# Six quads of the last stage in plain fp32 on an x that GpSimd splits afterwards, in a graph kernel on one Trainium2 core

## The chip, the cores and the metric

The kernel runs on one core of a Trainium2 chip. The metric is the device time of one execution in microseconds, and it is compared by the median of several runs.

## The reference, cut to what matters

The input is x (8192 x 128) and an adjacency matrix (8192 x 8192, fp32, 256 MB), of which about one entry in 256 is not zero; the kernel treats it as dense.

```python
d   = 1 / sqrt(sum(A, axis=-1))
z   = leaky_relu((d[:, None] * (A @ (d[:, None] * x))) @ W1 + b1, 0.1)
d2  = maximum(sq[:, None] + sq[None, :] - 2 * (z @ z.T), 0)     # sq = sum(z * z, axis=-1)
S   = exp(-sqrt(d2 + 1e-10) / 2)                                # kept for the 4 nearest of a row, else 0
A2  = S + A
e   = 1 / sqrt(sum(A2, axis=-1))
out = layernorm(x + (e[:, None] * (A2 @ (e[:, None] * x))) @ W2 + b2)
```

So A is multiplied twice, the second time with rows of x that are scaled by sums which need the four nearest neighbours of every row. The second product falls apart into A times the scaled x, and four gathered rows per row.

## The kernel before, in words

A row block b and a column block h are 512 wide (b, h from 0 to 15). A **quad** (b, h) is the 512 x 512 piece of A that they share, laid out for TensorE in DRAM, 1 MB and one DMA. A **tile** is 128 rows of x; a column block has four tiles, a **group** eight tiles, that is two column blocks.

Stages 1 and 2 (to about 1027 us in the span) form the row sums and the first product, and z. Stage 3 takes the 64 tiles one after the other: TensorE makes the 128 x 8192 scores of a tile, ScalarE copies them into SBUF, VectorE finds the eight largest and their places (`v.max`, `v.max_index`, semaphore `placed`). The rows of x of a group whose neighbours are known are scaled ("xg"), split into two parts that TensorE multiplies at its faster fp32r rate (a high half, rounded, and a low half, the rest), and written to DRAM three times: as fp32 (`xs_dram`), as high halves (`xh_dram`) and as low halves (`xl_dram`). The second product of row blocks 0 to 8 ("lights") with column blocks 0 to 13 is done beside stage 3; its sums lie in `acc_dram`.

**The last stage** does what is left of the second product: 124 quads in a fixed order, `tail`, made by `plan_tail` (line 115), u being the position in it. Row blocks 9 to 15 are "heavies" with 14 or 16 quads each, and the lights have two quads each (column blocks 14 and 15, h >= LAST). Row block 9 comes first; its first `OPEN_T` = 6 quads stand alone, then a light quad and a heavy one alternate. After that, two lights are put into each heavy block, at h = 5 and h = 10.

A quad takes one of two ways (function `quad`, line 961):
- **in halves**: ScalarE rounds the whole quad into `ah_t` (`round_t`, line 1194, operation at line 1197), VectorE subtracts to get the rest `al_t` in two parts (`rest_t`, line 1670, operation at line 1675), and TensorE does twelve fp32r matmuls (lines 987, 989, 993) with the high and low halves of x, which SP has loaded back from `xh_dram` and `xl_dram` (`load_xs`, line 721). The rests of the first two quads (`BY_POOL`) are made by GpSimd (line 1448).
- **plain**: four fp32 matmuls straight on the loaded quad (line 977). Before, these are the 32 quads of column blocks 14 and 15, which use the last group's `xg` in SBUF and wait until it is scaled (`xg_ok`).

Quads arrive in `RAW_T` = 7 buffers: SP issues the load of position u when the quad at u - 7 is done (`load_t`, line 715). The seven first loads and the halves of groups 0 to 2 are issued from line 727 on, behind waits for the last tile of stage 3; the others from line 741 on. In this trace the loads land in the order in which they are issued.

The last group's scale is made while the stage opens, in a chain over two engines, whose links stand at fixed positions of the loops: VectorE makes the distances (`last_chain_a`, line 1634), ScalarE takes root and exponential (`s_of_distances`, line 1099, at u = 2), VectorE the sums (`last_near_sums`, line 1643, at u = 3), ScalarE their root (`root_of_sums`, line 1106, at u = 3), VectorE the Newton step and the scaling of xg (`last_scale_of_rows` and `scale_last_xg`, at u = 4). GpSimd then writes xg to `xs_dram` (line 1453) and, when that has landed, issues 256 gathers of 128 rows with 512 bytes each (line 1464): 16 for each row block f in the order `FIN`, into three sets of buffers. ScalarE weighs them with the neighbours' S (`weigh`, line 1204, operation at line 1208), VectorE adds them, TensorE adds them to the block's sums and multiplies with W2, and so on to the layer norm. All that is tied to positions `FIN_AT`: ScalarE weighs the four parts of block f at u = FIN_AT[f] - 7 to FIN_AT[f] - 4. Each engine goes through its loop over u in order, so what waits at one position holds up all that stands behind it on that engine.

Of the kernel before, what the change touches and what calls it, by code (L numbers as in the profile page):

```python
# [39 lines left out]
RAW_T, HIGH_T = 7, 3  # L40
BY_POOL = 2
GX = 3
# [4 lines left out]
FIN_AT = (22, 28, 34, 41, 48, 55, 62, 69, 76, 83, 90, 97, 103, 109, 115, 123)  # L47
OPEN_T, SUM_AFTER, ACC_AT = 6, 4, (9, 20, 40)
SLOT = TB * BC
# [65 lines left out]
def plan_tail():  # L115

    lights = [(b, h) for b in LIGHTS for h in range(LAST, B)]
    quads = [(HB, h) for h in range(OPEN_T)]
    for h in range(OPEN_T, LAST):
        quads += [lights.pop(0), (HB, h)]  # L120
    quads += [(HB, h) for h in range(LAST, B)]
    for b in HEAVIES[1:]:
        for h in range(first_h(b), B):
            if h in (B // 3, 2 * B // 3) and lights:
                quads.append(lights.pop(0))
            quads.append((b, h))
    return quads


def build(nc, x, at, W1, b1, W2, b2, consts, out, xs_dram, xh_dram, xl_dram, acc_dram):  # L130
# [48 lines left out]
    with ctx:  # L179
# [114 lines left out]
        al_t = [sb(f"al_t{k}", [P, TB, BC], F32R, at=where) for k, where in enumerate(low_at)]  # L294

        def low_tile(t):

            return xsl[:, t] if t < (G - 2) * GT else xsh[:, t + GT]

# [97 lines left out]
        s_acc_x = sem("s_acc_x")  # L397
        acc_seeded = sem("acc_seeded")
        rnd_t = sem("rnd_t")
        al_pool = sem("al_pool")  # L400
        al_dve = sem("al_dve")
# [127 lines left out]

        plain = [h >= LAST for b, h in tail]  # L530
        halved = [u for u in range(len(tail)) if not plain[u]]
        place_of = {u: n for n, u in enumerate(halved)}

        def wait_rest(eng, u, part_=RESTS - 1):

            if place_of[u] < BY_POOL:
                eng.wait_ge(al_pool, place_of[u] + 1)
            else:
                eng.wait_ge(al_dve, RESTS * (place_of[u] - BY_POOL) + part_ + 1)

# [112 lines left out]
        def _(sp):  # L653
# [61 lines left out]
            def load_t(u):  # L715
# [3 lines left out]
                sp.dma_start(raw_t[u % RAW_T], at[b, h]).then_inc(ld_t[u % RAW_T], 16)  # L719

            def load_xs(g):
                low = g if g < G - 2 else G - 1
# [3 lines left out]

            sp.wait_ge(s_split, 32 * (G - 1))
            sp.wait_ge(placed, T - 1)
            for g in range(2):
                load_t(g)  # L730
                sp.wait_ge(gram, NE * (T - 1) + g + 1)
                load_xs(g)
            load_t(2)
            sp.wait_ge(gram, NE * T)
            load_t(3)
            load_xs(2)
            load_t(4)
            sp.wait_ge(prodb, pieces_before(G - 1))
            for u in range(5, RAW_T):
                load_t(u)  # L740
            for u in range(RAW_T, len(tail)):
                for g in range(3, G - 1):
                    if u == max(RAW_T, tail.index((HB, g * GT // TB)) - 1):
                        load_xs(g)
# [15 lines left out]
        def _(pe):  # L760
# [200 lines left out]
            def quad(u):  # L961
# [11 lines left out]
                if plain[u]:  # L973
                    pe.wait_ge(xg_ok, chain_of(G - 1, False))
                    pe.wait_ge(ld_t[u % RAW_T], 16 * (u // RAW_T + 1))
                    for k in range(TB):
                        i = pe.matmul(bank, xg[:, (h * TB + k) % GT], raw_t[u % RAW_T][:, k],  # L977
                                      start=from_zero and k == 0, stop=last and k == TB - 1,
                                      skip_group_check=True)
                    i.then_inc(prod_t, 1)  # L980
                    return
                pe.wait_ge(s_xs[h * TB // GT], 32)
                n = place_of[u]
                pe.wait_ge(rnd_t, n + 1)
                for k in range(TB):
                    t = h * TB + k
                    pe.matmul(bank, xsh[:, t], ah_t[n % HIGH_T][:, k], start=from_zero and k == 0, stop=False,  # L987
                              skip_group_check=True)
                    pe.matmul(bank, low_tile(t), ah_t[n % HIGH_T][:, k], start=False, stop=False, skip_group_check=True)
                for k in range(TB):  # L990
                    if k % (TB // RESTS) == 0:
                        wait_rest(pe, u, k * RESTS // TB)
                    i = pe.matmul(bank, xsh[:, h * TB + k], al_t[u % RAW_T][:, k], start=False, stop=False,
                                  skip_group_check=True)
# [33 lines left out]
        def _(act):  # L1028
# [211 lines left out]
            for u in range(len(tail)):  # L1240
                if not plain[u]:
                    round_t(u)
                for i, b in enumerate(ROWS_X):
                    if u == (FIN_AT[FIN.index(b - 2)] + 3 if b - 2 in HEAVIES else FIN_AT[0] - 8):
                        seed_heavy(i)
                if u == BY_POOL:
                    s_of_distances(G - 1)
                if u == BY_POOL + 1:
                    root_of_sums(G - 1)
                    act.wait_ge(placed, T)  # L1250
# [21 lines left out]
        def _(pool):  # L1272
# [198 lines left out]
        def _(v):  # L1471
# [308 lines left out]
```

## Time and profile before

| what | value |
|---|---|
| time, median of 3 runs (lowest, highest) | 2683.36 us (2681.94, 2683.89) |
| time of the profiled execution, and its span | 2679.84 us, 2678.0 us |
| last stage in the span | from 2233.6 us (first load) to the end, 444 us |
| busy share of the whole span | PE 92%, DVE 87%, ACT 60%, POOL 45% |
| granted clock of TensorE, mean of the span | 0.979 |

Times of rows count from the start of the span. PE is TensorE, DVE is VectorE, ACT is ScalarE, POOL is GpSimd, SP the engine that issues the loads (its queue is SPq). A granted clock of 1.00 is 2.4 GHz. DMA share is the mean busy share of the core's 16 DMA engines; it can come out a little over 1. "Idle before <-releaser" is the time in which the engine stood still just before an operation, and what ended it. Engine shares are means over stages with different limits, so the last stage is read from its own windows and timelines.

### The profile page before, as it was taken

Reading aid. Unit: us, or ns where it says so; the run is one execution under the profiler, and the core shown is the slowest. Engines: PE = TensorE matmul, PEld = TensorE weight load, DVE = VectorE, ACT = ScalarE, POOL = GpSimd, SP = SyncE. Lnnn points to the kernel's source line nnn. Section 1 sums busy time; section 2 is a strip of 40 time slices with the busy share of each in tenths; the row PEclk is TensorE's granted clock in tenths of the full one; section 3 lists DMA queues with packets and bytes.
Section 4 is the critical chain, followed back from the end, with each engine's and each line's share of the span. In section 5 each row is a group of like instructions: output and inputs, shape, how many; then the busy total and the mean of one; then the engine's idle time right before and its main releaser. Section 6 shows DMA issues by size and latency. Waiting matters only on the chain.

```text
span 2678.0 us, 29073 instructions
## 1 busy us (share of the span) xinstructions
PE 2456.8 (92%) x9356; PEld 1710.4 (64%) x9356; DVE 2319.3 (87%) x1411; ACT 1606.8 (60%) x1905; POOL 1193.2 (45%) x987
## 2 busy tenths in 40 slices
PE   0467999999999999899999999999999998899998
PEld 0133444444577777577778787877878775577776
DVE  7998889976788887999999999989999877488887
ACT  0000000000377776899998989889898876477776
POOL 0000000000000000067788888878787895777772
PEclk9678999999999999999999999999999999999999
DMA  9999999997699981035565555545555568999996
GB/s 383 421 405 402 399 421 421 421 421 291 236 374 345 341 329 52 0 114 170 147 170 147 168 149 141 175 135 177 146 173 148 168 179 320 398 400 402 400 402 244
DMA packets 147948, 718.58 MB, mean 268 GB/s; under 512 B 19024, under 2 KB 26960, under 8 KB 86608
## 3 DMA queue, kind: packets, MB, share of 16 engines
q1 hardware_dynamic: 124384, 670.49, 66.7%
q0 software_dynamic: 18800, 37.77, 5.7%
q10 hardware_dynamic: 4608, 8.39, 0.8%
q8 instruction: 79, 1.29, 0.2%
q14 instruction: 77, 0.63, 0.1%
HBM read 680.40 MB, written 36.18 MB: 268 GB/s over the span
## 4 chain that ended last, share of the span: by engine, by line
PE 59%; DMA 9%; issue 9%; DVE 9%; ACT 9%; POOL 3%; SPq 0%; ACTq 0%; POOLq 0%; DVEq 0%
PE PS L773 19%; PE PS L872 5%; PE PS L874 5%; PE PS L873 5%; DMA ring<-at 4%; ACT R L1147 3%; PE PS L840 3%; DMA R<-at 3%; PE PS L916 3%; PE PS L917 3%; PE PS L927 3%; PE PS L836 2%; PE PS L837 2%; PE PS L977 2%; DVE R L1629 2%
## 5 line engine op out<-in xcount | busy, mean ns | idle before, releaser
L1305 POOL TENSOR_TENSOR al<-ring,ah 128x1024 fp32r<-128x1024 f32 x264 | 643.7, 2439 | 181.6 <-ACT ah L1118 168.0
L1629 DVE MAX8 R<-R 128x8 f32<-128x8192 f32 x64 | 555.8, 8685 | 68.6 <-ACT R L1147 68.4
L1147 ACT ACTIVATE R<-PS 128x1024 f32<-128x1024 f32 x512 | 518.0, 1018 | 112.0 <-PE PS L880 82.6
L1632 DVE FIND_INDEX8 R<-R,R 128x8 uint32<-128x8192 f32 x64 | 555.9, 8685 | 0.3 <-issue 0.3
L1278 POOL CAST zst<-zh 128x128 fp32r<-128x128 f32 (+1 forms) x64 | 26.3, 411 | 1112.8 <-DVE zl L1564 811.1
L872 PE MATMUL PS<-zh,zst 128*128 128x512 f32 x1024 | 407.2, 398 | 28.5 <-ACT PS L1133 12.7
L874 PE MATMUL PS<-zh,zst 128*128 128x512 f32 x1024 | 400.4, 391 | 0.0
L873 PE MATMUL PS<-zl,zst 128*128 128x512 f32 x1024 | 400.2, 391 | 0.0
L1133 ACT ACTIVATE PS<-R 128x1024 f32<-128x1024 f32 x310 | 318.0, 1026 | 6.6
L1052 ACT ACTIVATE tiny<-rowsum 128x4 f32<-128x4 f32 x16 | 3.3, 205 | 482.1 <-DVE rowsum L1499 482.1
L773 PE MATMUL PS<-cache,R 128*128 128x512 f32 x584 | 263.5, 603 | 16.7 <-DMA cache<-at 11.3
L1489 DVE TENSOR_TENSOR R<-R,cache 128x2048 f32<-128x2048 f32 x106 | 242.9, 2292 | 19.8 <-DMA cache<-at 17.5
L872 PEld LDWEIGHTS PS<-zh,zst 128*128 128x128 f32 x1024 | 192.2, 188 | 96.9 <-ACT PS L1133 25.0
L1464 POOL DMA_INDIRECT R<-xs_dram,R x176 | 192.5, 1094 | 61.4 <-issue 52.7
L874 PEld LDWEIGHTS PS<-zh,zst 128*128 128x128 f32 x1024 | 192.3, 188 | 41.6
L873 PEld LDWEIGHTS PS<-zl,zst 128*128 128x128 f32 x1024 | 192.3, 188 | 39.8 <-issue 0.7
L773 PEld LDWEIGHTS PS<-cache,R 128*128 128x128 f32 x584 | 112.3, 194 | 157.6 <-issue 144.7
L773 PE MATMUL PS<-ring,R 128*128 128x512 f32 x384 | 175.9, 605 | 11.9 <-DMA ring<-at 6.4
L1572 DVE TENSOR_TENSOR al<-ring,ah 128x2048 fp32r<-128x2048 f32 x66 | 151.0, 2290 | 35.5 <-ACT ah L1045 33.0
L1489 DVE TENSOR_TENSOR R<-R,ring 128x2048 f32<-128x2048 f32 x72 | 165.0, 2291 | 11.6 <-DMA ring<-at 9.6
L987 PE MATMUL PS<-ah_t,xsh 128*128 128x512 f32 x368 | 153.3, 417 | 11.8 <-ACT ah_t L1197 11.6
L1045 ACT ACTIVATE ah<-ring 128x2048 fp32r<-128x2048 f32 x66 | 126.4, 1915 | 62.7 <-PE PS L840 59.9
(181 smaller groups left out, 4515.5 us busy)
## 6 DMA issues: line engine op xcount, KB each, us to landing
R<-at SPq DMA_DIRECT2D x160, 1024.0 KB, 14.7
ring<-at SPq DMA_DIRECT2D x148, 1024.0 KB, 9.4
ring<-at SPq DMA_DIRECT2D x264, 512.0 KB, 3.8
cache<-at SPq DMA_DIRECT2D x117, 1024.0 KB, 20.3
acc_dram<-R POOLq DMA_DIRECT2D x78, 256.0 KB, 5.7
raw_sq<-at SPq DMA_DIRECT2D x18, 1024.0 KB, 14.4
raw_z<-at SPq DMA_DIRECT2D x18, 1024.0 KB, 15.3
raw_ring<-at SPq DMA_DIRECT2D x17, 1024.0 KB
```

The source lines that it names most:

```text
L773: i = pe.matmul(PS[:, b % YB], xs[:, q * TB + k], slots_a[slot_of[n]][:, k], start=first and k == 0, stop=prod_at[b, q] == closed[b] and k ...
L872: pe.matmul(bank, zst[:, par, 0], zh[:, cols], start=not on_seed, stop=False, skip_group_check=True)
L873: pe.matmul(bank, zst[:, par, 0], zl[:, cols], start=False, stop=False, skip_group_check=True)
L874: i = pe.matmul(bank, zst[:, par, 1], zh[:, cols], start=False, stop=on_seed, skip_group_check=True)
L987: pe.matmul(bank, xsh[:, t], ah_t[n % HIGH_T][:, k], start=from_zero and k == 0, stop=False, skip_group_check=True)
L1133: act.activation(pair(False, 0, c), sq_row[c], ACT.Copy).then_inc(seeded, 1)
L1147: act.activation(score[j % 2][:, c * EC:(c + 1) * EC].rearrange("p (b c) -> p b c", b=2), pair(first, j, c), ACT.Copy).then_inc(copied, 1)
L1305: pool.tensor_tensor(al[:, k % SPLIT], raw[k % RAW], ah[:, k % SPLIT].bitcast(F32), ALU.subtract)\
L1464: pool.indirect_dma_start(gx[f % GX][:, j, m], None, xs_dram, bass.IndirectOffsetOnAxis(ap=sidx[:, FIN[f] * TB + j, m:m + 1], axis=0))\
L1489: v.tensor_tensor(total.rearrange("p (k c) -> p k c", c=BC), other, slots_a[slot_of[n]], ALU.add)\
L1629: v.max(top[:, j], score[j % 2]).then_inc(dve3, 1)
L1632: v.max_index(place[:, j], top[:, j], score[j % 2]).then_inc(placed, 1)
```

## The change

It has three parts, all in the last stage.

- The first six quads (block 9, column blocks 0 to 5) become plain: fp32 matmuls on x in fp32. So SP loads groups 0 to 2 of x as fp32 from `xs_dram` into `xsh` (`load_xf`), 0.5 MB each with rows of 512 bytes, instead of their halves from two tensors. Later row blocks need the halves of these groups too: GpSimd makes them in place, the high half into `xsl` as soon as the group is there, the low half into `xsh` when the two quads that use the group are done. The two names are exchanged for these tiles (`high_tile`, `low_tile`). GpSimd makes no rests of quads any more.
- The first quad in halves is now position 6 (`FIRST`), and the lights begin at position 8. ScalarE takes both roots and the exponential of the last group directly behind the rounding at position 6, before the rounding at 7. VectorE makes the sums at position 7 and the scaling at 8. The halves of group 3 are loaded ahead of loads 5 and 6; those of groups 4 to 6 one position earlier relative to their first quad.
- The remaining twelve lights are put in after every sixth heavy quad, not at h = 5 and h = 10. `FIN` and `FIN_AT` stay.

```diff
-BY_POOL = 2
+OPEN_PLAIN, LIGHT_STEP = 6, 6
-OPEN_T, SUM_AFTER, ACC_AT = 6, 4, (9, 20, 40)
+FIRST, OPEN_T, SUM_AFTER, ACC_AT = OPEN_PLAIN, OPEN_PLAIN + 2, 4, (9, 20, 40)
...
     quads += [(HB, h) for h in range(LAST, B)]
+    passed = 0
     for b in HEAVIES[1:]:
         for h in range(first_h(b), B):
-            if h in (B // 3, 2 * B // 3) and lights:
+            if passed % LIGHT_STEP == LIGHT_STEP // 2 and lights:
                 quads.append(lights.pop(0))
             quads.append((b, h))
+            passed += 1
...
+        swapped = OPEN_PLAIN * TB
+        def high_tile(t):
+            return xsl[:, t] if t < swapped else xsh[:, t]
         def low_tile(t):
-            return xsl[:, t] if t < (G - 2) * GT else xsh[:, t + GT]
+            return xsh[:, t] if t < swapped else xsl[:, t] if t < (G - 2) * GT else xsh[:, t + GT]
...
-        plain = [h >= LAST for b, h in tail]
+        plain = [h >= LAST or (b == HB and h < OPEN_PLAIN) for b, h in tail]
...
+            def load_xf(g):
+                sp.dma_start(xsh[:, g * GT:(g + 1) * GT].bitcast(F32),
+                             xs_dram[g * GT * P:(g + 1) * GT * P].rearrange("(t p) d -> p t d", p=P))                  .then_inc(s_xf[g], 16)
...
             for g in range(2):
                 load_t(g)
                 sp.wait_ge(gram, NE * (T - 1) + g + 1)
-                load_xs(g)
+                load_xf(g)
             load_t(2)
             sp.wait_ge(gram, NE * T)
+            load_xf(2)
             load_t(3)
-            load_xs(2)
             load_t(4)
+            load_xs(OPEN_PLAIN * TB // GT)
             sp.wait_ge(prodb, pieces_before(G - 1))
             for u in range(5, RAW_T):
                 load_t(u)
             for u in range(RAW_T, len(tail)):
-                for g in range(3, G - 1):
-                    if u == max(RAW_T, tail.index((HB, g * GT // TB)) - 1):
+                for g in (*range(OPEN_PLAIN * TB // GT + 1, G - 1),):
+                    if u == max(RAW_T, tail.index((HB, g * GT // TB)) - 2):
                         load_xs(g)
...
                 if plain[u]:
-                    pe.wait_ge(xg_ok, chain_of(G - 1, False))
+                    if h >= LAST:
+                        pe.wait_ge(xg_ok, chain_of(G - 1, False))
+                    else:
+                        pe.wait_ge(s_xf[h * TB // GT], 16)
...
-                pe.wait_ge(s_xs[h * TB // GT], 32)
+                if h < OPEN_PLAIN:
+                    pe.wait_ge(xf_split, h * TB // GT + 1)
+                else:
+                    pe.wait_ge(s_xs[h * TB // GT], 32)
...
-                if u == BY_POOL:
+                if u == FIRST:
                     s_of_distances(G - 1)
-                if u == BY_POOL + 1:
                     root_of_sums(G - 1)
                     act.wait_ge(placed, T)
...
-            for u in range(BY_POOL):
-                pool.wait_ge(rnd_t, u + 1)
-                pool.tensor_tensor(al_t[u % RAW_T][:, :, :], raw_t[u % RAW_T], ah_t[u % HIGH_T][:, :, :].bitcast(F32),
-                                   ALU.subtract).then_inc(al_pool, 1)
+            for g in range(OPEN_PLAIN * TB // GT):
+                tiles = slice(g * GT, (g + 1) * GT)
+                pool.wait_ge(s_xf[g], 16)
+                pool.wait_ge(gram, NE * T)
+                pool.tensor_copy(xsl[:, tiles], xsh[:, tiles].bitcast(F32)).then_inc(xf_high, 1)
+                pool.wait_ge(xf_high, g + 1)
+                pool.wait_ge(prod_t, tail.index((HB, (g + 1) * GT // TB - 1)) + 1)
+                pool.tensor_tensor(xsh[:, tiles], xsh[:, tiles].bitcast(F32), xsl[:, tiles].bitcast(F32),
+                                   ALU.subtract).then_inc(xf_split, 1)
...
             last_chain_a(lk)
-            for u in range(BY_POOL, len(tail)):
-                if u == BY_POOL + 1:
+            for u in range(FIRST, len(tail)):
+                if u == FIRST + 1:
                     last_near_sums(lk)
-                if u == BY_POOL + 2:
+                if u == FIRST + 2:
                     last_scale_of_rows(lk)
                     scale_last_xg(G - 1)
```

## Rows read from the trace of the kernel before

**Rows 1.** Windows of the last stage: us, then busy time of each engine, clock, DMA share, GB/s
```profile
2250.00:2260.00 10.00, 6.13 (x21) 4.04 (x19) 9.67 (x8) 2.09 (x2) 2.79 (x1) 0.84 1.02 422
...
2277.00:2640.00 363.00, 350.95 (x1429) 248.41 (x1428) 282.47 (x522) 249.34 (x399) 278.38 (x256) 1.00 1.02 400
...
2651.00:2678.00 27.00, 17.07 (x62) 9.84 (x60) 12.57 (x40) 7.27 (x13) 0.00 (x0) 0.89 0.06 23
```

**Rows 2.** Timeline of SP's queue, opening loads: start, us, line, transfer
```profile
2233.62 0.34 SPq L719 DMA_DIRECT2D R<-at  x1
...
2250.05 4.35 SPq L719 DMA_DIRECT2D R<-at  x2
```

**Rows 3.** DMA issues by line: count, size, median us to landing
```profile
xs_dram<-R SPq DMA_DIRECT2D x7, 512.0 KB, 3.5
...
gx_last<-xs_dram,R POOLq DMA_INDIRECT x80, 5.9
```

**Rows 4.** Timeline of ACT, opening: start, us, line, operation, [idle before <-releaser]
```profile
2259.82 0.23 ACT L1102 ACTIVATE R<-R 128x32 f32<-128x32 f32 x1 [5.77 <-DVE R L1640]
...
2260.07 1.28 ACT L1104 ACT_TABLE_LOAD   x1
...
2261.36 0.23 ACT L1104 ACTIVATE R<-R 128x32 f32<-128x32 f32 x1
...
2269.64 1.92 ACT L1197 ACTIVATE ah_t<-R 128x2048 fp32r<-128x2048 f32 x1 [1.12 <-DMA R<-at]
```

**Rows 5.** Timeline of DVE, opening
```profile
2259.79 2.35 DVE L1675 TENSOR_TENSOR al_t<-R,ah_t 128x1024 fp32r<-128x1024 f32 x2
...
2262.06 0.17 DVE L1646 TENSOR_REDUCE tiny<-R 128x8 f32<-128x32 f32 x1
...
2262.27 0.17 DVE L1647 TENSOR_TENSOR tiny<-tiny,rowsum 128x8 f32<-128x8 f32 x1
...
2265.78 0.20 DVE L447 RECIPROCAL tiny<-tiny 128x8 f32<-128x8 f32 x1
...
2267.13 1.23 DVE L1658 TENSOR_TENSOR R<-R,tiny 128x1024 f32<-128x1024 f32 x1
```

**Rows 6.** Timeline of POOL: write of the last group, first and 240th gather
```profile
2268.66 0.99 POOL L1453 DMA_DIRECT2D xs_dram<-R  x1 [15.88 <-DVE R L1658]
...
2277.74 1.06 POOL L1464 DMA_INDIRECT R<-xs_dram,R  x1 [8.09 <-DMA xs_dram<-R]
...
2609.52 0.94 POOL L1464 DMA_INDIRECT gx_last<-xs_dram,R  x1 [0.30 <-issue]
```

**Rows 7.** Groups by line and form, 2170 us to the end: busy, mean ns | idle before
```profile
L1464 POOL DMA_INDIRECT R<-xs_dram,R x176 | 192.5, 1094 | 61.4 <-issue 52.7
...
L1464 POOL DMA_INDIRECT gx_last<-xs_dram,R x80 | 85.9, 1074 | 24.4 <-issue 23.5 <-DVE R L1689 0.9
...
L1305 POOL TENSOR_TENSOR al<-ring,ah 128x1024 fp32r<-128x1024 f32 x22 | 54.2, 2473 | 1.7 <-ACT ah L1118 0.9
```

**Rows 8.** Timeline of ACT near the end
```profile
2622.32 0.40 ACT L1208 ACTIVATE gx_last<-gx_last,sval_t 128x128 f32<-128x128 f32 x1 [0.43 <-ACT R L1226]
...
2623.51 3.71 ACT L1197 ACTIVATE ah_t<-R 128x2048 fp32r<-128x2048 f32 x2
...
2635.60 0.20 ACT L1219 ACTIVATE small<-small 128x4 f32<-128x4 f32 x1 [2.73 <-DVE small L1718]
```

**Rows 9.** Timeline of DVE near the end
```profile
2625.45 2.36 DVE L1675 TENSOR_TENSOR al_t<-R,ah_t 128x1024 fp32r<-128x1024 f32 x2
...
2635.40 0.17 DVE L1718 TENSOR_SCALAR small<-small 128x4 f32<-128x4 f32 x1
```

**Rows 10.** Chain of waits: one plain quad (4 matmuls, 4 weight loads)
```profile
2274.15 3.43 PE PS L977 x8
```

**Rows 11.** Timeline of PE: one quad in halves, up to the operation behind it
```profile
2616.71 0.39 PE L987 MATMUL PS<-ah_t,xsh 128*128 128x512 f32 x1
...
2619.43 1.05 PE L1004 MATMUL PS<-ident,R 128*128 128x128 f32 x8
```

More of the change, by code:

```diff
@@ L398, in build @@
         acc_seeded = sem("acc_seeded")
+        s_xf = [sem(f"s_xf{k}") for k in range(OPEN_PLAIN * TB // GT)]
+        xf_high = sem("xf_high")
+        xf_split = sem("xf_split")
         rnd_t = sem("rnd_t")
-        al_pool = sem("al_pool")
         al_dve = sem("al_dve")
@@ L528, in build @@
         n_heavy = [f + 1 - n_light[f] for f in range(B)]
-        plain = [h >= LAST for b, h in tail]
+        plain = [h >= LAST or (b == HB and h < OPEN_PLAIN) for b, h in tail]
+        assert not any(plain[FIRST:OPEN_T])
         halved = [u for u in range(len(tail)) if not plain[u]]
@@ L534, in wait_rest @@
         def wait_rest(eng, u, part_=RESTS - 1):
[L536 to L539, printed above, removed]
+            eng.wait_ge(al_dve, RESTS * place_of[u] + part_ + 1)
         def wait_halves_free(eng, u):
@@ L727, in _ @@
             sp.wait_ge(s_split, 32 * (G - 1))
+            sp.wait_ge(s_xg, 16 * (G - 1))
             sp.wait_ge(placed, T - 1)
@@ L973, in quad @@
                 if plain[u]:
-                    pe.wait_ge(xg_ok, chain_of(G - 1, False))
+                    if h >= LAST:
+                        pe.wait_ge(xg_ok, chain_of(G - 1, False))
+                    else:
+                        pe.wait_ge(s_xf[h * TB // GT], 16)
                     pe.wait_ge(ld_t[u % RAW_T], 16 * (u // RAW_T + 1))
                     for k in range(TB):
-                        i = pe.matmul(bank, xg[:, (h * TB + k) % GT], raw_t[u % RAW_T][:, k],
+                        t = h * TB + k
+                        rows = xg[:, t % GT] if h >= LAST else xsh[:, t].bitcast(F32)
+                        i = pe.matmul(bank, rows, raw_t[u % RAW_T][:, k],
                                       start=from_zero and k == 0, stop=last and k == TB - 1,
@@ L986, in quad @@
                     t = h * TB + k
-                    pe.matmul(bank, xsh[:, t], ah_t[n % HIGH_T][:, k], start=from_zero and k == 0, stop=False,
+                    pe.matmul(bank, high_tile(t), ah_t[n % HIGH_T][:, k], start=from_zero and k == 0, stop=False,
                               skip_group_check=True)
@@ L992, in quad @@
                         wait_rest(pe, u, k * RESTS // TB)
-                    i = pe.matmul(bank, xsh[:, h * TB + k], al_t[u % RAW_T][:, k], start=False, stop=False,
+                    i = pe.matmul(bank, high_tile(h * TB + k), al_t[u % RAW_T][:, k], start=False, stop=False,
                                   skip_group_check=True)
```

## The prediction

> **What bounds the kernel now.** I read the windows of the last stage first. From 2277 to 2640 us the sixteen DMA engines are full (share 1.02) at 400 GB/s, and just before, at 422 GB/s [rows 1]. PE is busy for 351 of these 363 us too, but the ends of its matmuls are modelled; the DMA engines have no idle share at all, so I take their loads as the pace. They end near 2651 us, and a drain of 27 us follows with the DMA share at 0.06 [rows 1]. The queue of SP comes next: the first adjacency load goes out at 2233.62, when tile 62 has been searched, and the eighth at 2250.05, when the first quad is done [rows 2]; between them nothing waits for a quad. The edit leaves the start of that queue where it is, so its gain in DMA can only be bytes.
>
> Two things hang on the last group's scaled rows, and the timelines show them: the first plain quad of column block 14, and the write of these rows to DRAM, behind which POOL issues all 256 gathers.
>
> **The change part by part.** A change within 0.2% (5.4 us) is about what a measurement of this kernel can't tell from none.
>
> *Bytes.* Three groups of x come as fp32 (0.5 MB each) instead of as two halves (1 MB). A megabyte (1.049 MB decimal) takes 2.48 us at 422 GB/s. The new source has rows of 512 bytes, and no load of that kind stands here. The gathers move rows of that size: 256 of 64 KB are 16.8 MB. Of the 363 us x 400 GB/s = 145.2 MB, the other 128.4 MB would need 304 us at 422 GB/s; so the gathers cost 59 us, or 1.84 us for 0.5 MB [rows 1]. Bounds: 1.24 us (bytes alone) and 3.5 us, the landing of the 0.5 MB write with rows of 512 bytes [rows 3]. I take 1.84, the row that has them under the same load. Saved: 3 x (2.48 - 1.84) = 1.9 us; by the bounds, 3.7 saved or 3.1 lost. The loads still come in one queue, and by my order it never runs dry: seven adjacency loads and two pairs of halves are queued before any quad must end.
>
> *The chain to the gathers.* Square root, exponential and second root of the last group move from positions 2 and 3 to position 6, and the scaling on DVE from 4 to 8. Before, load 7 lands at 2269.6, where ACT's idle time ends [rows 4], as the last of 8 loads and 4 pairs, 12 MB. Now load 6 stands behind 6 loads, one pair and three fp32 groups: 4 MB less, three groups more, so it lands 4 x 2.48 - 3 x 1.84 = 4.4 us earlier, at 2265.2, and load 7 (one pair and itself later) at 2270.2. Then:
> - ACT rounds quad 6 in 1.92, takes the root in 0.23, loads the table in 1.28, takes the exponential in 0.23: 2268.9 [rows 4].
> - DVE meanwhile makes the rest of quad 6 (2.36, as the first row of [rows 5]) until 2269.5, then the sums, 0.4 from the start of the one row to the end of the other [rows 5]: 2269.9.
> - ACT now waits for these sums with the rounding of quad 7 queued behind. A second table load (1.28) and a root (0.2) follow. If the load needs no sums it is over at 2270.2, else at 2271.2; no row tells which. The rounding ends at 2272.3 or 2273.3.
> - DVE: rest of quad 7, 2.36; Newton step, 1.35 from the one start to the other; scaling, 1.23 [rows 5]. The rows are scaled at 2277.3 or 2278.3; I take the middle, 2277.8, against 2268.4 before: 9.4 us later.
> - The write goes out 0.3 us behind, and the first gather 9.1 us behind that [rows 6]. DMA is as full then as before, so I keep this. The same 0.5 MB landed in 3.5 us with free engines [rows 3] instead of about 8: that is the bound below, 4.6 us less.
>
> The table switch is 1.28 us of load with the exponential starting 0.01 us behind it [rows 4]. The Trainium skill (ScalarE: Activation LUTs, "What ACT_TABLE_LOAD costs") adds a drain of about 1.38 us to each switch of set. By that rule the two switches, which now both lie on this chain, would make it 2.8 us longer and the sum 2688.7; this trace shows no such gap.
>
> *What 9.4 us do to the gathers.* They are a stream of their own: 256 issues in 278 us busy and 86 us idle, less the 8.1 us wait ahead of the first, are 1.39 us each, and of the idle time only 0.9 us is put down to DVE, the wait for a free buffer [rows 6, 7]. POOL is issuing all the time, and nothing lets it catch up. The spare time is smallest for the 240th gather, the last of row block 14: issued at 2609.52 [rows 6], it lands 5.9 us later by the median [rows 3], at 2615.4, and ACT weighs it from 2622.32 [rows 8]. That is 6.9 us. Shifted by 9.4, it lands at 2624.8, and ACT stands 2.5 us longer than before. Behind ACT wait the roundings of quads 112 and 113 (2623.51, [rows 8]); DVE takes the rest of quad 112 at 2625.45, the moment it is rounded, and shows no idle mark until the variance at 2635.40 [rows 9], for which ACT waits until 2635.60 [rows 8]; ACT then runs on with gaps of half a microsecond. No slack takes the 2.5 us up. The 1.9 us of DMA don't come off: ACT would only arrive earlier and wait longer.
>
> *Work on PE.* A plain quad is 3.43 us [rows 10], one in halves 2.72 [rows 11]; six exchanged cost 4.3 us. They fall into an opening in which quads wait for their loads (PE busy 6.13 of 10 us, clock 0.84, between its levels of 1.2 and 2.4 GHz, [rows 1]), so I cost them at nothing; without that cover the end would be 4.3 us later.
>
> *POOL.* Two subtractions on quads go. Three copies and three subtractions on x come (2.5 us each, the subtraction of this shape in [rows 7]; a copy reads half as much, and I give it no more), each subtraction behind two quads. They stand ahead of the write and the gathers in POOL's queue. The last waits for quad 5, whose load lands 2.5 us before load 6: 2262.7, plus 3.43 and 2.5, is 2268.6, under the scaling at 2277.8. Cost nothing; if the quad were ten microseconds later, it would set the gathers' start. Later quads need these halves only from position 22.
>
> *ACT, DVE and order.* Six roundings and four rests fewer in the opening: idle there already, nothing. Lights every sixth heavy quad: the same 124 quads and bytes; from position 103 on the order is unchanged, and each row block still ends before its fixed place for gathering. Nothing.
>
> **Sum.** 2.5 us on the profiled execution's 2679.84 is 2682.3. The median of the three runs lies 3.5 us above that execution, so I predict 2685.9.
>
> **Rivals.**
> 1. *The gathers are early enough* (0.20). If the chain loses under 6.9 us, for instance because the write lands in 3.5 us (9.4 - 4.6 = 4.8), nothing waits at block 14, and the end follows the loads: 1.9 to 3.7 us earlier, 2679.7 to 2681.5. Against it: the DMA share at that time.
> 2. *Rows of 512 bytes are slow* (0.24). At 3.5 us each the three groups push loads 6 and 7 back by 3 x 1.66 = 5.0 us. The chain is then 14.4 us late, or 14.9 with the later table load, and the end 7.5 to 8.0 us later: 2691.4. It decides from about 2.8 us a group: from there on the chain is over 12.3 us late and the end over 5.4. For it: they are the only new kind of load and stand at the very front. Against it: as a write, such rows landed as fast as any.
> 3. *A switch of ACT's table costs more than its load* (0.03). If it held ACT for as long again as the load's 1.28 us, the two on the chain would make it 12.0 us late and the end 5.1: 2688.4. The 0.01 us between load and exponential [rows 4] speaks against it. The drain that the Trainium skill's page names above would be of this kind.
> 4. *The drain gets shorter* (0.07). If evenly spread lights leave ACT, DVE and PE less behind the loads, part of PE's 10 idle us in the last 27 [rows 1] goes; half of it and the bytes are 6.9 us: 2676.5. Against it: the order from position 103 on.
>
> **How the numbers follow.** The forecast, a stream of gathers that binds by a few microseconds, has 0.46. Its own range is 2682 to 2689. Over 8 in 10 the range runs from 2678.5 (rival 1 and a little of 4) to 2692.0 (rival 2 at its upper bound). Faster by over 0.2%: rival 4 and a fifth of rival 1, 0.11. Slower: rivals 2 and 3 and the edge of the forecast, 0.30. Within: 0.59.
>
> **What would show it.** The scaling of the last group ends near 2277.8 and the first gather starts near 2287; the three fp32 loads land about 1.8 us behind what is queued ahead of them; ACT waits for a gather at block 14, where before it waited for none; loads end 1 to 2 us earlier than before. I am wrong if the first gather starts before 2285 or after 2290, if no weighing waits, or if the DMA share falls below 1 between 2250 and 2640.

## The result, and the profile after

The kernel before has a median of 2682.78 us in five runs (2681.94 to 2683.89), the changed one 2692.92 us (2688.53 to 2697.45): a ratio of 1.0040, with a 95% interval of 1.0025 to 1.0055. That is slower by 10.1 us where I had put 2.5 us, and 0.9 us beyond the end of my range; my likeliest case was "no change". The profiled execution of the changed kernel took 2688.53 us (span 2686.7), the fastest of its five.

The last stage doesn't begin at the same time in every execution: its first load goes out at 2233.62 before [rows 2] and at 2232.20 after, and between 2232 and 2239 in the runs below. So I count from that first load ("+44.1"). The stage takes 444.4 us before and 454.5 after.

Windows of the changed kernel, the first two as in [rows 1], the third to its later end (time; busy PE, PEld, DVE, ACT, POOL; clock; DMA share; GB/s):

```profile
2250.00:2260.00 10.00, 9.89 (x23) 4.12 (x23) 9.85 (x3) 0.00 (x0) 5.54 (x3) 1.00 1.02 421
2277.00:2640.00 363.00, 345.83 (x1376) 242.69 (x1377) 271.36 (x503) 242.08 (x391) 278.72 (x248) 0.99 1.00 390
2651.00:2687.00 36.00, 25.37 (x101) 16.32 (x99) 19.33 (x49) 15.74 (x28) 1.83 (x2) 0.93 0.21 78
```

The opening is as full as before, at 421 GB/s. In the long window the rate has gone from 400 to 390 GB/s, so loads are no longer the pace everywhere, and POOL is still issuing gathers at 2651 us, where before it had been done for 17 us. POOL's timeline, with two of the three subtractions of the opening, the write, the first and the last gather, a few gathers near 2600 us, and at 2628.02 the 240th, which the prediction rests on:

```profile
2257.79 2.35 POOL L1474 TENSOR_TENSOR xsh<-xsh,xsl 128x1024 fp32r<-128x1024 f32 x1 [3.88 <-PE PS L996]
...
2265.33 2.39 POOL L1474 TENSOR_TENSOR xsh<-xsh,xsl 128x1024 fp32r<-128x1024 f32 x1 [4.21 <-PE PS L996]
2277.54 0.99 POOL L1479 DMA_DIRECT2D xs_dram<-R  x1 [9.82 <-DVE R L1684]
2287.28 1.06 POOL L1490 DMA_INDIRECT R<-xs_dram,R  x1 [8.75 <-DMA xs_dram<-R]
...
2601.43 1.85 POOL L1490 DMA_INDIRECT R<-xs_dram,R  x1 [0.30 <-issue]
...
2605.06 0.94 POOL L1490 DMA_INDIRECT R<-xs_dram,R  x1 [0.30 <-issue]
2606.31 1.93 POOL L1490 DMA_INDIRECT gx_last<-xs_dram,R  x1 [0.31 <-issue]
...
2628.02 0.94 POOL L1490 DMA_INDIRECT gx_last<-xs_dram,R  x1 [0.30 <-issue]
...
2651.71 1.42 POOL L1490 DMA_INDIRECT R<-xs_dram,R  x1 [0.30 <-issue]
```

The first gather starts at 2287.28; I had 2287.1. ACT, at the opening, at a weighing of the first row block, at the four weighings that need the 240th gather (2631.03), and at the last four:

```profile
2263.95 1.91 ACT L1219 ACTIVATE ah_t<-R 128x2048 fp32r<-128x2048 f32 x1 [23.62 <-DMA R<-at]
...
2267.54 1.28 ACT L1131 ACT_TABLE_LOAD   x1
2270.27 0.21 ACT L1131 ACTIVATE tiny<-tiny 128x8 f32<-128x8 f32 x1 [1.44 <-DVE tiny L1673]
...
2313.54 0.40 ACT L1230 ACTIVATE R<-R,sval_t 128x128 f32<-128x128 f32 x1 [3.55 <-DMA R<-xs_dram,R]
...
2631.03 0.40 ACT L1230 ACTIVATE gx_last<-gx_last,sval_t 128x128 f32<-128x128 f32 x1 [0.43 <-DMA gx_last<-xs_dram,R]
...
2657.93 0.40 ACT L1230 ACTIVATE R<-R,sval_t 128x128 f32<-128x128 f32 x1
```

ACT waits for gathers from the very first block on. The groups of gathers and of weighings show how much (answering to [rows 7]):

```profile
L1490 POOL DMA_INDIRECT R<-xs_dram,R x176 | 198.0, 1125 | 62.1 <-issue 52.4 <-DMA xs_dram<-R 8.8 <-DVE R L1715 0.9
L1490 POOL DMA_INDIRECT gx_last<-xs_dram,R x80 | 90.2, 1127 | 24.4 <-issue 23.5 <-DVE R L1715 0.9
L1230 ACT ACTIVATE R<-R,sval_t 128x128 f32<-128x128 f32 x176 | 55.9, 389 | 25.8 <-DMA R<-xs_dram,R 23.2 <-ACT R L1248 2.6
L1230 ACT ACTIVATE gx_last<-gx_last,sval_t 128x128 f32<-128x128 f32 x80 | 25.5, 390 | 22.5 <-DMA gx_last<-xs_dram,R 21.2 <-ACT R L1248 1.3
```

The weighings wait 23.2 + 21.2 = 44.4 us for gathers, and a gather's issue takes 1.13 us instead of 1.09 and 1.07. The last four weighings start at +415.5 before (2649.09) and at +425.7 after (2657.93), 10.2 us later, and in the two traces the span ends 28.9 and 28.8 us behind their start. That can be split into three terms: the first gather is 11.0 us later (+55.1 against +44.1 [rows 6]); from the first gather to the last it is 364.4 us, not 354.2 (the last one started at 2631.97 before), 10.2 us more; and the last four weighings used to start 17.1 us behind the issue of the last gather and now start 6.2 us behind it, 10.9 us less. 11.0 + 10.2 - 10.9 = 10.3. The terms add up by the way they are taken, so this shows where the time went and not yet why.

Block 14, on which the prediction rests, says more. Its last gather, the 240th, is issued at +395.8 (2628.02) instead of +375.9 [rows 6], 19.9 us later, and the weighings that need it start at +398.8 (2631.03) instead of +388.7 [rows 8], 10.1 us later, as much as the end. ACT waits 8.3 us for gathers within this block, where before it waited for none.

VectorE's timeline shows two more things, for later: instructions that are drawn out beside POOL's subtractions (here 2.26 and 4.04 us), and the rests beside which the gathers above are slow. Each row of a rest is two instructions. Taken singly, the rest at 2606.20 has its first half done at 2607.42, and the gather that started beside it at 2606.31 ends at 2608.24, 0.82 us later. It is so throughout: 108 of the changed kernel's 256 gathers take over 1 us, and all of these but the first end 0.81 to 0.83 us behind a VectorE instruction that was running when they started, 71 of them behind a rest. So a slow gather waits out the one instruction that it met, and no more.

```profile
2257.93 2.26 DVE L1665 TENSOR_TENSOR R<-R,sq 128x32 f32<-128x32 f32 x1
...
2265.89 4.04 DVE L1701 TENSOR_TENSOR al_t<-R,ah_t 128x1024 fp32r<-128x1024 f32 x2 [4.65 <-ACT ah_t L1219]
...
2601.24 2.36 DVE L1701 TENSOR_TENSOR al_t<-R,ah_t 128x1024 fp32r<-128x1024 f32 x2
...
2606.20 2.36 DVE L1701 TENSOR_TENSOR al_t<-R,ah_t 128x1024 fp32r<-128x1024 f32 x2 [1.94 <-ACT ah_t L1219]
```

### The profile page after: what moved, and what is told of

Same layout as the page of the kernel before. It is cut to its first block, busy times and chain, and to the rows that moved or that the text cites. A ratio compares the mean times of both kernels' runs of the same rounds, so it can differ in the third digit from the quotient of the medians.

```text
span 2686.7 us, 29014 instructions
## 1 busy us (share of the span) xinstructions
PE 2465.1 (92%) x9332; PEld 1708.3 (64%) x9332; DVE 2314.3 (86%) x1403; ACT 1594.8 (59%) x1899; POOL 1204.1 (45%) x991
## 4 chain that ended last, share of the span: by engine, by line
PE 53%; POOL 10%; issue 10%; DVE 9%; ACT 9%; DMA 7%; SPq 1%; ACTq 0%; POOLq 0%; DVEq 0%
PE PS L787 19%; POOL R L1490 6%; PE PS L886 5%; PE PS L888 5%; PE PS L887 5%; DMA ring<-at 4%; ACT R L1169 4%; PE PS L930 3%; PE PS L854 3%; PE PS L931 3%; PE PS L941 3%; DVE R L1655 2%; PE PS L850 2%; PE PS L851 2%; POOL gx_last L1490 2%
## 5 line engine op out<-in xcount | busy, mean ns | idle before, releaser
L886 PE MATMUL PS<-zh,zst 128*128 128x512 f32 x1024 | 407.1, 398 | 28.6 <-ACT PS L1155 12.7
L1490 POOL DMA_INDIRECT R<-xs_dram,R x176 | 198.0, 1125 | 62.1 <-issue 52.4
L1701 DVE TENSOR_TENSOR al_t<-R,ah_t 128x1024 fp32r<-128x1024 f32 x114 | 136.3, 1237 | 52.5 <-ACT ah_t L1219 52.4
## 6 DMA issues: line engine op xcount, KB each, us to landing
R<-at SPq DMA_DIRECT2D x160, 1024.0 KB, 10.2
```

The lines of the kernel that those rows point to most:

```text
L886: pe.matmul(bank, zst[:, par, 0], zh[:, cols], start=not on_seed, stop=False, skip_group_check=True)
L1490: pool.indirect_dma_start(gx[f % GX][:, j, m], None, xs_dram, bass.IndirectOffsetOnAxis(ap=sidx[:, FIN[f] * TB + j, m:m + 1], axis=0))\
```

## The experiments

Theory 1: the gather stream, later and slower, sets the end. Theory 2: the 512-byte rows of the fp32 loads cost the time. Theory 3: the new places of the light quads do. Theory 4, on why the stream is slower: VectorE's rests hold up the gathers' issue.

The table is read from SP's and POOL's timelines of each run's trace: first gather, length of the stream (start of the first gather to the end of the last), issue of quad 110's load, gathers issued ahead of it, time from there to the end, the end, and ACT's waits for gathers. Numbers with a plus count from the first load.

```
run                        gather  stream  load110  ahead  from there   end    waits
before                      +44.1   356.1   +366.4   233      77.9     +444.4    0
after                       +55.1   365.8   +370.2   222      84.3     +454.5   44.4
after_again                 +55.1   366.9   +372.4   222      86.3     +458.7   45.3
early_chain                 +46.8   363.6   +362.4   222      85.8     +448.2   12.7
before_late_chain           +49.5   361.7   +365.9   225      83.2     +449.0    7.6
before_lights_sixth         +44.3   366.3   +375.5   233      78.0     +453.4    0
before_new_order            +43.7   364.6   +367.9   229      78.2     +446.2    2.5
after_short_rests           +50.6   323.2   +367.6   251      71.6     +439.2    0
early_split_later           +44.3   368.8   +363.1   222      86.7     +449.8   13.3
early_quarter_rests         +46.9   331.8   +369.9   250      78.8     +448.7    0
after_quarter_rests         +56.1   332.4   +368.1   240      78.8     +446.8    7.6
early_half_quarter_rests    +47.8   338.8   +370.0   245      77.9     +447.9    0
early_half_quarter_split    +41.9   340.9   +371.2   249      77.9     +449.1    0
early_fifth_quarter_rests   +47.5   355.6   +365.6   231      78.0     +443.5    0
```

**1. The chain moved forward in the changed kernel.**

```diff
 # ScalarE, u == FIRST
+    s_of_distances(G - 1); root_of_sums(G - 1); act.wait_ge(placed, T)
     round_t(u)
-    s_of_distances(G - 1); root_of_sums(G - 1); act.wait_ge(placed, T)
 # VectorE, ahead of the loop over u
+last_near_sums(lk); last_scale_of_rows(lk); scale_last_xg(G - 1)
```

> The changed kernel, but ScalarE takes square root, exponential and root of the last group ahead of the first rounding, and VectorE its sums, Newton step and scaling ahead of the first rest; the six plain quads and the light quads stay. Theory 1 (the late gather stream sets the end): first gather near 2277 instead of 2287, ScalarE's weighing waits for gathers for under 2 us in all instead of 23, time 2679 to 2683, no slower than the kernel before. Theory 2 (the 512-byte rows of the three fp32 loads cost the time): still 2690 or more, whenever the gathers start. Theory 3 (the new places of the light quads cost it): still 2690 or more.

Measured: 2685.84 us, 1.0016 (1.0007 to 1.0025) against the kernel before. VectorE's chain, and the groups as above:

```profile
2258.16 2.01 DVE L1664 TENSOR_SCALAR R<-R 128x32 f32<-128x32 f32 x1
...
2265.61 2.12 DVE L452 TENSOR_SCALAR tiny<-tiny 128x8 f32<-128x8 f32 x1
```

```profile
L1490 POOL DMA_INDIRECT R<-xs_dram,R x176 | 195.2, 1109 | 62.1 <-issue 53.3 <-DMA xs_dram<-R 8.7
...
L1230 ACT ACTIVATE R<-R,sval_t 128x128 f32<-128x128 f32 x176 | 55.6, 389 | 6.4 <-DMA R<-xs_dram,R 3.8 <-ACT R L1248 2.6
L1230 ACT ACTIVATE gx_last<-gx_last,sval_t 128x128 f32<-128x128 f32 x80 | 25.4, 388 | 10.6 <-DMA gx_last<-xs_dram,R 8.9 <-ACT R L1248 1.7
```

8.3 us earlier gathers take 7 us off the changed kernel's 2692.92, and waits fall from 44.4 to 12.7 us. The fp32 loads, the plain opening and the order are all still there, so theories 2 and 3 don't carry these 7 us. But it is still 3.8 us slower than before, and not the 2679 to 2683 that I expected: it is 4.0 us ahead at quad 110, and then waits for the gathers of the last blocks, since the stream is still 364 us long (the 240th is 10.2 us late, 3.3 more than its spare time). Two tiny instructions of the chain took 2 us instead of 0.17, beside POOL's subtractions.

**2. The chain moved back in the kernel before**, two positions (`BY_POOL + 2`, `+ 3`, `+ 4` in place of `BY_POOL`, `+ 1`, `+ 2`).

> The kernel before with nothing changed but the place of the last group's chain: each of its four steps on ScalarE and VectorE two quads later, so the gathers start some 8 to 10 us later; opening, loads and light quads as before. Theory 1: weighing waits for gathers appear, and the time rises by 6 to 10 us to 2689 to 2693, as in the changed kernel. Theories 2 and 3: nothing they blame is in this kernel, so 2683 within 2 us.

Measured: 2685.33 us, 1.0008 (0.9999 to 1.0017): 3.3 us, inside what a measurement can't tell from nothing, and half of the least that I expected. The gathers came 5.4 us later, and the waits are there where none had been, all 7.6 us of them in block 14:

```profile
L1464 POOL DMA_INDIRECT gx_last<-xs_dram,R x80 | 89.3, 1116 | 24.4 <-issue 23.2 <-DVE R L1689 1.2
...
L1208 ACT ACTIVATE gx_last<-gx_last,sval_t 128x128 f32<-128x128 f32 x80 | 25.3, 388 | 9.3 <-DMA gx_last<-xs_dram,R 7.6 <-ACT R L1226 1.7
```

The trace allows a closer look than the medians. By my forecast 5.4 us would have cost nothing, since block 14 has 6.9 us to spare. But the stream got slower as well, 361.7 us instead of 356.1, so the 240th gather is 11.6 us late (+387.5). Less 6.9 that is 4.7, and the weighings that need it start 4.7 us later (+393.4), the traced stage ends 4.6 us later. So block 14 works as I had forecast; what the forecast lacked is that the stream slows down, here with the old order and the old opening.

**3. The light quads alone**, in the kernel before, every sixth but with the old opening of six (`passed % 6 == 3` in `plan_tail`).

> The kernel before with nothing changed but the light quads among the heavy ones, every sixth instead of two fixed places in each block; the opening still takes six heavy quads before the first light one. Theory 1: 2683 within 2 us, no weighing waits. Theory 3: 2688 to 2693.

Measured: 2691.33 us, 1.0037 (1.0025 to 1.0049). This is what theory 3 expected, and I had not. But there are no waits for gathers in it (table), and the loss builds up evenly until quad 110 (+375.5 against +366.4), not at the end. VectorE's waits name it:

```profile
DVE al_t L1677 <- ACT ah_t L1199: 59.5, 26, 6.6
DVE R L1698 <- PE PS L1006: 27.9, 7, 6.5
```

In the kernel before, the second of these waits was

```profile
DVE R L1696 <- PE PS L1004: 10.6, 6, 4.5
```

VectorE waits 27.9 us (10.6 before) for the gathered products of light blocks on PE, with the rests of the next quads queued behind. Plain quads stand in this order at places 41, 55, 69, 76 and 90, exactly where a light block's product is due; of these the old order has only 55, the changed kernel's only 69. (The expectation of the next run but one lists them without 41 and calls them all light.)

**4. The changed kernel with short rests.**

```diff
-v.tensor_tensor(al_t[u % RAW_T][:, ks], raw_t[u % RAW_T][:, ks], ...
+v.tensor_tensor(al_t[u % RAW_T][:, ks, 0:64], raw_t[u % RAW_T][:, ks, 0:64], ...
```

TensorE's third product is cut to the same 64 of 512 columns, so the output leaves out the low half of A in the others.

> The changed kernel in which VectorE's rest of each halved quad covers 64 of the 512 columns (and TensorE's third product the same 64), so the output leaves out the low half of A in the other columns. Theory 4 (a gather's issue on GpSimd takes 0.94 us alone and up to 2 us beside a VectorE subtraction of two SBUF operands, so the rests pace the stream): gathers' mean issue near 1.0 us instead of 1.13, the 256 of them in some 330 to 340 us instead of 366, no weighing waits after the first blocks, time 2678 to 2683. If the pace has another cause (descriptor ring, DMA load): mean still over 1.1 us, stream still 360 us or more, time still 2688 or more.

Measured: 2675.41 us, 0.9971 (0.9960 to 0.9983).

```profile
L1490 POOL DMA_INDIRECT R<-xs_dram,R x176 | 169.0, 960 | 61.4 <-issue 51.8 <-DMA xs_dram<-R 8.0 <-DVE R L1715 1.5
L1490 POOL DMA_INDIRECT gx_last<-xs_dram,R x80 | 76.5, 956 | 24.4 <-issue 23.5 <-DVE R L1715 0.9
```

Theory 4 holds for the stream: 0.96 us each, 323 us in all, no waits, although the gathers start only 4.5 us earlier than in the changed kernel. The time itself proves less, as this kernel also has less VectorE and TensorE work in it (71.6 us behind quad 110).

**5. The changed kernel's whole order in the kernel before** (`OPEN_T = 8` as well).

> The kernel before with the changed kernel's order of quads, all of it (eight heavy quads before the first light one, then lights every sixth heavy quad); loads, halves and the last group's chain as before. In the order run before this one light quads 55, 69, 76 and 90 stood exactly where a light block's gathered products are queued on TensorE; in this order only 69 does. If the changed order costs the changed kernel its time: 2689 or more and VectorE's waits on TensorE's gathered products (light sums) near 28 us, as in that run. If that cost belongs to those four places alone and not to this order: 2681 to 2685, those waits under 18 us.

Measured: 2684.03 us, 1.0006 (0.9997 to 1.0015), and VectorE's waits:

```profile
DVE al_t L1677 <- ACT ah_t L1199: 67.9, 31, 9.1
DVE R L1698 <- PE PS L1006: 13.9, 5, 5.6
```

So experiment 3 measured its own order; the changed kernel's order costs next to nothing by itself, and theory 3 falls as a direct cost. What it does leave is a stream of 364.6 us instead of 356.1 in these two traces. It is mostly hidden here because the gathers start early: the 240th is 7.7 us late, 0.8 more than its spare time, and the traced stage ends 1.8 us later.

**6. GpSimd's split behind the write**, in the early-chain kernel (groups 1 and 2 of the loop in the diff, moved behind the write to `xs_dram`).

> The early-chain kernel with GpSimd's split of the second and third fp32 group moved behind its write of the last rows, into the 8.7 us in which it waits for that write. Theory (a GpSimd subtraction of two SBUF operands holds up every VectorE instruction beside it until it ends: in the early-chain run two small ones took 2.01 and 2.12 us instead of 0.17): the chain is 3.5 to 4 us shorter, first gather near 2275.5 instead of 2279.4, and since the gather stream sets the end the time falls by 2.5 to 4 us to 2682 to 2683.5. If the two long instructions have another cause they stay long, and the time stays 2685 to 2687.

Measured: 2686.53 us, 1.0010 (1.0001 to 1.0019), no gain.

```profile
2267.08 0.99 POOL L1481 DMA_DIRECT2D xs_dram<-R  x1 [13.93 <-DVE R L1688]
2268.07 2.11 POOL L1471 CAST xsl<-xsh 128x1024 fp32r<-128x1024 f32 x1
2270.26 3.23 POOL L1474 TENSOR_TENSOR xsh<-xsh,xsl 128x1024 fp32r<-128x1024 f32 x1
...
2278.93 1.06 POOL L1494 DMA_INDIRECT R<-xs_dram,R  x1 [0.16 <-issue]
```

The mechanism is right, as L452 of the chain takes 0.17 us here, and the write goes out at +32.5 instead of +37.1. But beside VectorE's rests a copy takes 2.11 us instead of 1.04 and a subtraction 3.23 instead of 2.39, and the split itself now holds back the first gather (+44.3). The stream is 368.8 us long, so the 2.5 us gained at its start are lost on the way.

**7 and 8. Rests in four pieces** (`RESTS = 4`), with the early chain and with the changed kernel's late one.

> The early-chain kernel with each rest in four instructions of 512 columns instead of two of 1024. If a gather's issue has to wait only for the VectorE instruction it meets, and can slip in between two: mean issue under 1.08 us instead of 1.12, stream under 350 us instead of 364, weighing waits gone, time 2675 to 2681. If it has to wait for as long as rests follow one another: mean issue 1.11 or more, the stream and the time as in the early-chain run or longer by VectorE's 240 more instructions (2686 to 2692).

> The changed kernel with nothing but each rest in four instructions of 512 columns instead of two of 1024; its late chain and its order stay, so the gathers start near 2287 as in the changed kernel. Theory 1 with theory 4 (the late and slow gather stream is the whole loss): stream near 332 us instead of 366 and over near 2620, weighing waits only in the first three blocks (under 15 us instead of 42), time 2684 to 2688, 5 to 9 us under the changed kernel. If the loss lies elsewhere in the changed kernel: 2691 or more, as VectorE has only got more instructions.

Measured: 2684.97 us, 1.0013 (1.0003 to 1.0023), and 2684.01 us, 1.0007 (0.9998 to 1.0016). The second is the key: one constant that touches neither opening, chain nor order takes 8.9 us off the changed kernel. Its groups:

```profile
L1490 POOL DMA_INDIRECT R<-xs_dram,R x176 | 175.3, 996 | 62.3 <-issue 53.0 <-DMA xs_dram<-R 9.0 <-DVE R L1715 0.3
...
L1230 ACT ACTIVATE R<-R,sval_t 128x128 f32<-128x128 f32 x176 | 55.7, 389 | 9.2 <-DMA R<-xs_dram,R 6.6 <-ACT R L1248 2.6
```

Gathers slip in between shorter instructions, and the waits go from 44.4 to 7.6 us. With the early chain nothing waits, yet almost nothing is gained (0.9 us on experiment 1); my 2675 to 2681 was wrong. A window of that run near its end, and the same stretch of the kernel before:

```profile
2600.00:2640.00 40.00, 40.00 (x178) 30.48 (x176) 37.08 (x91) 30.62 (x49) 9.35 (x10) 1.00 0.98 387
2600.00:2640.00 40.00, 39.60 (x180) 30.30 (x179) 36.67 (x70) 31.30 (x47) 26.83 (x24) 1.00 1.02 402
```

PE is busy for all of 40 us and DVE for 37.1, while the DMA share is a little lower; but PE and DVE were as busy in the kernel before. This fits an end that no longer hangs on the gathers, and doesn't show which of the others sets it. What the table does show is what the fast gathers cost in the early-chain kernels: quad 110's load goes out at +362.4 with 222 gathers ahead of it and at +369.9 with 250, by my estimate 0.3 us per gather. Behind that load the stage takes 78 to 79 us in every run that waits for gathers 8 us or less, except the late chain's, whose waits lie there, and the short rests'.

**9, 10, 11. Looking for the place between** (early chain; four pieces for the first 60 halved quads; the same with two subtractions behind the write; four pieces for the first 24).

> The early-chain kernel with rests in four pieces for the first 60 halved quads and in two behind them. In the early-chain run the quads were 5 us ahead of the kernel before until quad 110 and lost 8 us to gathers; with four pieces throughout the waits were gone, but the lead too, as the gathers took their share of the DMA time earlier and the end was left to VectorE and TensorE. Expected if that is so: stream near 348 us, over near 2628, no or few weighing waits, quad 110 issued 1 to 3 us ahead of the kernel before, time 2678 to 2682. If the pieces or the opening cost something of their own: 2684 or more.

> The same, with the subtractions of the second and third fp32 group on GpSimd moved behind its write of the last rows (their copies stay ahead of it). Without a GpSimd subtraction beside them no small VectorE instruction of the chain takes 2 us, and the two subtractions, some 6.5 us beside the rests, fit into the wait for the write: first gather near 2276, 3 to 4 us earlier than in the early-chain run, and the time 0 to 2 us under the run before this one. If the moved subtractions hold the gathers up instead, the first gather stays at 2279 and the time with it.

> The early-chain kernel with rests in four pieces for the first 24 halved quads alone. From the traces so far: a stretch without weighing waits lasts 78 us from the issue of quad 110's load to the end, whatever is ahead of it, and each gather that is issued before that load puts it off by about 0.3 us. With 24 quads in pieces the stream should gain some 8 us on the early-chain run (last gather near 402 us behind the first load instead of 410), with about 228 gathers ahead of quad 110: its load 364 us behind the first one (before: 366.4), weighing waits under 4 us, time 1 to 3 us under the kernel before. If the gathers have no just-in-time place between too many and too late: 2682 to 2685 like its neighbours.

Measured: 2682.42 us, 0.9999 (0.9990 to 1.0008); 2683.57 us, 1.0008 (0.9999 to 1.0017); and 2681.04 us, 0.9991 (0.9982 to 1.0000). The first two still had 245 and 249 gathers ahead of quad 110 and wait for none. In the split's run the first gather came 5.9 us earlier than without it (+41.9), and that didn't help either. The third landed where the table's two rules put it: 231 gathers, load at +365.6, 78.0 us from there.

```profile
L1496 POOL DMA_INDIRECT R<-xs_dram,R x176 | 191.2, 1086 | 63.5 <-issue 53.1 <-DMA xs_dram<-R 10.1 <-DVE R L1721 0.3
...
L1236 ACT ACTIVATE R<-R,sval_t 128x128 f32<-128x128 f32 x176 | 55.6, 389 | 2.6 <-ACT R L1254 2.6
L1236 ACT ACTIVATE gx_last<-gx_last,sval_t 128x128 f32<-128x128 f32 x80 | 25.4, 388 | 2.1 <-ACT R L1254 2.1
```

It is the best of these, 12 us under the changed kernel's median, but its 1.3 us under the kernel before can't be told from nothing.

**12. The changed kernel again.**

> The changed kernel once more, beside the kernel before on this chip, for a second trace of it. If the slow gather stream is the kernel's own and not one execution's: stream 360 to 370 us again, weighing waits of 25 us or more, first gather 54 to 56 us behind the first load; time 2690 to 2695. If the 366 us were chance: stream near 356 us, waits under 15 us.

Measured: 2695.78 us, 1.0045 (1.0031 to 1.0059), with the same late and slow stream (+55.1, 366.9 us) and 45.3 us of waits. The slow stream is the kernel's own.

## Why the prediction was wrong

**Bytes: right, as far as seen.** Load 6 was put 31.6 us behind the first load (2265.2) and landed 31.75 us behind it (2263.95 - 2232.20). At 3.5 us a group it would have been 36.6: rival 2 falls, the 512-byte rows cost no more than I took.

**The chain: right but for two rows.** The first gather came at 2287.28 for 2287.1, but that is luck: the whole stage began 1.4 us earlier in this execution. Against the first load the gather is 11.0 us later instead of 9.4. The rest of quad 6 took 4.04 us, not the 2.36 of [rows 5], beside POOL's third subtraction, and the first gather came 9.7 us behind the write, not 9.1. That subtraction is the very one I had costed at nothing since it ended before the scaling: it does end, but it draws out VectorE's link of the chain. The table load started at 2267.54, before the sums, which settles the point I had left open; the exponential started 0.01 us behind its load, so rival 3 falls too. That rival 2's 2691.4 lies nearest to the measured time is chance.

**The step that failed is "What 9.4 us do to the gathers".** How block 14 stops ACT was right: in experiment 2, lateness less 6.9 us of spare time gave the 4.7 us that its weighings lost. The size was wrong. I put the 240th gather 9.4 us late, 2.5 more than the spare time; it was 19.9 us late, and its weighings and the end came 10.1 us later. (19.9 less 6.9 would be 13.0; the gather landed 2.7 us behind its issue, not 5.9.) Of the 19.9 us, 11.0 are the later start and 8.9 the slower stream up to there. Two things in that step were wrong.
- I kept the pace of [rows 7] for the stream, 1.39 us a gather, and took it that VectorE delays POOL only by the 0.9 us of idle time put down to it. The delay lies inside the issues: a gather takes 0.94 us alone and up to twice that beside a rest (1.93 at 2606.31, beside the rest from 2606.20). Before, 58 gathers waited out a rest and lost 26.8 us by it, counted over 0.94 each; after, 71 did and lost 37.0. These 10.2 us are the 10.2 by which the whole stream is longer. I had costed the order at nothing here. In experiment 5 the order alone made the stream 8.5 us longer; in experiment 2 the late chain alone made it 5.6 us longer. The two don't add up to 10.2, so how much of it is the order's is open.
- I took the spare time from the kernel before and shifted only the gathers against it. But the quads came earlier too: quad 34's load went out at +114.6 instead of +119.7. So ACT waited from the first block on (3.55 us at 2313.54), not only at block 14. By quad 60 this lead was gone (+206.6 against +206.1).

Experiments 1, 4 and 8 take the loss away from three sides, by an earlier start and by two faster streams, and the count of gathers that wait out a rest gives the slower stream its size; that is why I call it shown. Why more gathers do so in the changed kernel is not.

**Cover for PE: not tested by itself.** From 2250 us PE is now busy for 9.89 of 10 us instead of 6.13, and load 6 isn't late for it. With the early chain the six plain quads still leave quad 110's load 4.0 us ahead of the kernel before, so their 4.3 us don't show up there. No version with the plain opening got clearly ahead: with fast gathers quad 110's load comes late, and behind it the stage takes about the 78 us that it took before. What sets these 78 us I don't know; no run has PE's part alone. Of my signs, the first gather fell within 2285 to 2290 and ACT did wait, but the loads didn't end earlier (the last went out at +418.8 instead of +408.7), and the DMA share fell below 1: from 2600 to 2640 it was 0.91 at 341 GB/s, where the kernel before had 1.02 at 402. The loads, which I had as the pace, were waiting for quads, and these, by my reading, for ACT.

## What to carry to other kernels

A stream of small issues on one engine that never idles is a bound of its own: compare its first and last issue with the first and last use, and take its pace as a distribution (0.94 alone, 1.93 beside a neighbour's instruction), not as a mean that survives a reordering. Idle time is not the only mark of a neighbour: here its delay sat inside the issues' own durations. Spare time is a difference of two times, so a change that speeds the consumer uses it up as surely as one that delays the producer. Where a mean is set by collisions, cutting the other engine's instructions into shorter pieces can be worth more than moving the chain: here one constant took back 8.9 of 10 us.

## What the runs showed of the hardware

- Gathers' issue on GpSimd and VectorE's rests hold each other up one way only: the gather takes 0.94 to 2.01 us, the rest keeps its 1.22 us (median, with or without a gather beside it; the longest beside one took 1.30). A gather that waits ends 0.82 us behind the rest that it met (median of 71 in the changed kernel). In four pieces of 0.68 us instead of two of 1.22, the gathers' mean falls from 1.12 to 0.99 us (early-chain runs). The Trainium skill (SBUF — State Buffer, "Who interferes with whom") says that a VectorE instruction with two SBUF inputs contends with a GpSimd instruction that reads SBUF; the subtractions and copies of the next point agree, and in these traces a gather's issue behaves the same way.
- GpSimd's own subtraction does hold VectorE up, even small instructions: 2.01, 2.12 and 2.26 us instead of 0.17 to 0.19, until the subtraction ends. Two of the three are `tensor_scalar`, which the same section counts among the operations that can take the shared ports; the third has two inputs. Where both are long, each waits out the other's running instruction: in the changed kernel the first half of a rest takes 2.91 us and ends 1.1 us behind the subtraction, which keeps its 2.39, and the second half keeps 1.21 (together the 4.04 above). In experiment 6 they take turns, and both are drawn out: rests of 1.99 and 2.05 us, copies of 2.11 and 2.03, subtractions of 3.23 and 3.22.
